# Graph network kernel on one Trainium2 core: message sums into two column halves of TensorE, a 128-partition accumulator, and a merged, pipelined node update

## What is computed

```
layer 0:  g = (h @ W) * dis ;  agg = segment_sum(g[src], dst) ;  x += h + gelu(dis * (agg + g) + b)
layer 1:  msg = relu([h[src], h[dst], edge] @ W1 + b1) @ W2 + b2
          agg = segment_sum(msg, dst)
          x  += relu([agg, h] @ U1 + c1) @ U2 + c2
```

## Time and profile before

| | us |
|---|---|
| median of 3 runs | 2646.51 |
| the three runs | 2646.51, 2634.43, 2647.69 |
| the profiled execution, its own time | 2642.74 |
| its span, first to last instruction | 2641.0 |
| busy: PE, PE weight loads, DVE, POOL, ACT | 2303.5, 1988.5, 1827.3, 1829.3, 1130.6 |

### The profile page before, as it was taken

The page is one execution under the profiler, slowest core; times in us unless marked ns, Lnnn a source line. Parts: engine busy times, 40 slices in busy tenths (PEclk is TensorE's granted clock), DMA queues, the critical chain, the costliest instruction groups (busy, mean ns, idle before and its releaser), DMA issues.

```text
span 2641.0 us, 71244 instructions
## 1 busy us (share of the span) xinstructions
PE 2303.5 (87%) x22534; PEld 1988.5 (75%) x22535; DVE 1827.3 (69%) x5068; ACT 1130.6 (43%) x2326; POOL 1829.3 (69%) x1684
## 2 busy tenths in 40 slices
PE   2357999999994499999999999999999999999988
PEld 1246778777873378888888888888888888888874
DVE  8876777777786676666666666666666666666642
ACT  0016778878883133333333333333333333333321
POOL 2647777777770067777777777777777777777770
PEclk7569999999997699999999999999999999999986
DMA  2011111111120323333233333233223333332331
GB/s 65 1 27 27 27 28 27 28 28 28 28 28 2 71 50 64 66 65 65 63 64 65 66 65 65 65 65 65 64 63 65 66 66 66 66 65 65 64 49 24
DMA packets 349624, 134.26 MB, mean 51 GB/s; under 512 B 306107, under 2 KB 323361, under 8 KB 349473
## 3 DMA queue, kind: packets, MB, share of 16 engines
q1 hardware_dynamic: 297506, 79.11, 13.3%
q0 software_dynamic: 51968, 53.32, 10.8%
HBM read 124.78 MB, written 7.49 MB: 50 GB/s over the span
## 4 chain that ended last, share of the span: by engine, by line
PE 34%; POOL 32%; issue 13%; DVE 10%; DMA 6%; SPq 3%; ACT 1%; DVEq 1%; POOLq 0%; PEldq 0%; ACTq 0%
POOL rows L573 32%; PE psum L1306 8%; PE psum L1337 6%; PE psum L1458 4%; PE psum L1423 3%; DMA rows<-a_rows,idx 3%; PE psum L1432 2%; DMA idx<-src_by_tile 2%; PE psum L1470 2%; PE psum L1443 2%; PE psum L1327 2%; DVE H L949 1%; SPq L445 1%; PE psum L1414 1%; PE psum L1515 1%
## 5 line engine op out<-in xcount | busy, mean ns | idle before, releaser
L573 POOL DMA_INDIRECT rows<-a_rows,idx x1176 | 1284.1, 1092 | 496.0 <-issue 337.7
L573 POOL DMA_INDIRECT rows<-g_rows,idx x448 | 463.1, 1034 | 169.4 <-issue 135.0
L1115 ACT ACTIVATE hT<-psum 128x392 bf16<-128x392 f32 x1120 | 496.7, 502 | 139.2 <-PE psum L1337 131.8
L949 DVE TENSOR_SCALAR H<-Y,node_cmp 128x512 bf16<-128x512 f16 (+1 forms) x1372 | 383.0, 353 | 192.8 <-ACT Y L1150 192.8
L1458 PE MATMUL psum<-edge_index,H 128*128 128x192 bf16 x4802 | 430.3, 247 | 32.0 <-DVE H L949 32.0
L1306 PE MATMUL psum<-work,hT 128*128 128x192 bf16 x3430 | 447.1, 248 | 0.3 <-ACT hT L1115 0.3
L1458 PEld LDWEIGHTS psum<-edge_index,H 128*128 128x128 bf16 x4802 | 397.1, 99 | 54.9 <-issue 52.2
L1337 PE MATMUL psum<-Z,one_lo 128*128 128x392 f16 x1120 | 359.3, 342 | 28.8 <-DVE Z L827 28.6
L1423 PE MATMUL psum<-wb,eoT 128*128 128x64 f32 x3136 | 380.3, 275 | 0.0
L1306 PEld LDWEIGHTS psum<-work,hT 128*128 128x128 bf16 x3430 | 317.7, 99 | 70.6 <-issue 3.5
L1423 PEld LDWEIGHTS psum<-wb,eoT 128*128 128x128 f32 x3136 | 368.9, 193 | 0.1
(11 more groups left out here) (237 smaller groups left out, 2140.3 us busy)
## 6 DMA issues: line engine op xcount, KB each, us to landing
work<-in_edge_attr_dram SPq DMA_DIRECT2D x390, 128.0 KB
rows<-a_rows,idx POOLq DMA_INDIRECT x1176
Z<-slot_code SPq DMA_DIRECT2D x98, 128.0 KB, 3.0
rows<-g_rows,idx POOLq DMA_INDIRECT x448
idx<-src_by_tile SPq DMA_DIRECT2D x203, 4.0 KB, 1.8
wb<-b_rows SPq DMA_DIRECT2D x196, 16.0 KB, 1.9
g_rows<-Y SPq DMA_DIRECT2D x1, 1600.0 KB, 7.1
a_rows<-Y SPq DMA_DIRECT2D x1, 1600.0 KB, 7.2
```

The costliest lines, as they stand in the source:

```text
L573: pool.indirect_dma_start(out=rows[:, k, t, :], out_offset=None, in_=table, in_offset=bass.IndirectOffsetOnAxis(ap=idx[:, k, t:t + 1], axis=0)
L949: ins = V.tensor_scalar(pick[:, b, cols], slot_src[:, cols], node_cmp[:, b:b + 1], None, ALU.is_equal)
L1115: nc.scalar.activation(counts[:, j % 2, :, t * SLOTS:(t + 1) * SLOTS], psum[:, t % 4, 0:KEYS].rearrange("p (h m) -> p h m", m=SLOTS), ACT.Copy
```

## The change

1. `sum_messages` sums the even tiles into partitions 0 to 63 of the PSUM bank and the odd ones into 64 to 127, in the same sixteen weight loads and matmuls. `acc` has 128 partitions, and DVE's addition takes all of them.
2. The node update has two stages. `w_agg` is `w_msg2 @ w_upd1[0:64]`, stacked twice (so that it also adds the two halves) and repeated in both column halves; `w_node` holds `w_upd1[64:128]` for `h`, and in row 0 `b_msg2 @ w_upd1[0:64]` for the count of edges, which is now row 0 of `hT`. The hidden layer comes out twice, on 128 partitions, and `w_out` is half of `w_upd2`, stacked twice. Hidden and output products follow each other in one loop, two chunks apart, and SP stores each eight blocks as they are ready.
3. The merged weights are made in the preparation, behind layer 0's table: a transpose and two products on PE, seven small copies on ACT. SP's list of weights grows from 11 to 15 DMAs.
4. The output bias is added to `X` by DVE between the layers, in the place where DVE cleared `acc`. POOL clears the upper part of `hT` and the 128 partitions of `acc` there, while the layer's first steps run, and SP reads the counts back there instead of in the preparation.

```diff
-        w_msg2 = sb("w_msg2", [D + 1, D])
-        w_upd1 = sb("w_upd1", [P, D])
-        b_upd1 = sb("b_upd1", [D, 1])
-        w_upd2 = sb("w_upd2", [D + 1, D])
+        w_msg2 = sb("w_msg2", [D, D])
...
+        w_node = sb("w_node", [P, P])
+        w_agg = sb("w_agg", [P, P])
...
-        acc = sb("acc", [D + 1, NP])
+        acc = sb("acc", [P, NP])
@@ SyncE
-            sp.wait_ge(s_acc0, 1)
-            sp.dma_start(acc[D:D + 1, :], cnt_dram.rearrange("(a b) p -> a (b p)", a=1)).then_inc(s_cntr, 16)
...
+            sp.wait_ge(s_hrow, 1)
+            sp.dma_start(hT[0:1, :], cnt_dram.rearrange("(a b) p -> a (b p)", a=1)).then_inc(s_cntr, 16)
             sp.wait_ge(s_codec, 1)
...
-            sp.wait_ge(s_u3c, NB // T + 1)
-            sp.dma_start(out[0:NFULL * P, :].rearrange("(b p) d -> p b d", p=P), Y[:, 0:NFULL, :]).then_inc(s_out, 16)
+            for c in range(0, NB, T):
+                sp.wait_ge(s_u3c, c // T + 1)
+                full = min(T, NFULL - c)
+                if full > 0:
+                    sp.dma_start(out[c * P:(c + full) * P, :].rearrange("(b p) d -> p b d", p=P), Y[:, c:c + full, :]).then_inc(s_out, 16)
@@ GpSimd
             nc.gpsimd.memset(acc[:, :], 0.0).then_inc(s_acc0, 1)
+            nc.gpsimd.memset(w_node[0:D, :], 0.0).then_inc(s_acc0, 1)
...
+            pool.wait_ge(s_stT, 1)
+            nc.gpsimd.memset(hT[0:D, :], 0.0).then_inc(s_hrow, 1)
+            pool.wait_ge(s_stT, NB // T + 1)
+            nc.gpsimd.memset(acc[:, :], 0.0).then_inc(s_acc1, 1)
             pool.wait_ge(s_mode1, 1)
@@ VectorE
-                        V.tensor_tensor(acc[0:D, bass.ds(b0, W)], acc[0:D, bass.ds(b0, W)], psum[0:D, 4, 0:W],
+                        V.tensor_tensor(acc[:, bass.ds(b0, W)], acc[:, bass.ds(b0, W)], psum[:, 4, 0:W],
...
-            link(V.memset(acc[0:D, :], 0.0))
+            bu3 = wide(b_upd2[:, :].rearrange("p (b d) -> p b d", b=1), 1, NB)
+            link(V.tensor_tensor(X[:, :, :], X[:, :, :], bu3, ALU.add))
+            dve.wait_ge(s_acc1, 1)
             dve.wait_ge(s_split_a, 2)
...
-            for c in range(0, NP, 512):
-                m = min(512, NP - c)
-                q = c // 512
-                dve.wait_ge(s_u1, q + 1)
-                V.tensor_copy(hT[0:D, c:c + m], psum[0:D, q % 2, 0:m]).then_inc(s_u1c, 1)
-
-            dve.wait_ge(s_u1, NP // 512 + 1)
-            V.memset(acc[D:D + 1, :], 1.0).then_inc(s_one_row, 1)
@@ ScalarE
             sqrt_var(0)
+            act.wait_ge(s_wT, 1)
+            for half in (slice(0, D), slice(D, 2 * D)):
+                nc.scalar.activation(w_msg2T[:, half], psum[0:D, 7, 0:D], ACT.Copy).then_inc(s_wTc, 1)
+            act.wait_ge(s_wagg, 1)
+            for half in (slice(0, D), slice(D, 2 * D)):
+                nc.scalar.activation(w_agg[:, half], psum[:, 7, 128:128 + D], ACT.Copy).then_inc(s_wready, 1)
+                nc.scalar.activation(w_node[0:1, half], psum[0:1, 7, 256:256 + D], ACT.Copy).then_inc(s_wready, 1)
+            nc.scalar.activation(w_out[:, :], w_upd2[:, :], ACT.Copy, scale=0.5).then_inc(s_wready, 1)
...
-                nc.scalar.activation(acc[0:D, c:c + m], psum[0:D, 2 + q % 2, 0:m], ACT.Relu, bias=b_upd1[:, :]).then_inc(s_u2c, 1)
+                nc.scalar.activation(acc[:, c:c + m], psum[:, q % 4, 0:m], ACT.Relu, bias=b_upd1[:, :]).then_inc(s_u2c, 1)
@@ TensorE
+            TT.transpose(psum[0:D, 7, 0:D], w_msg2[:, :], ident[0:D, 0:D]).then_inc(s_wT, 1)
+            pe.wait_ge(s_wTc, 2)
+            TT.matmul(psum[:, 7, 128:128 + D], w_msg2T[:, :], w_upd1[:, :], start=True, stop=True)
+            TT.matmul(psum[0:1, 7, 256:256 + D], b_msg2[:, :], w_upd1[:, :], start=True, stop=True).then_inc(s_wagg, 1)
+            pe.wait_ge(s_wready, 5)
...
-                        ins = TT.matmul(psum[0:D, 4, 0:W], msg[:, k % 2, t, :], eo[:, k, t, D:2 * D],
-                                        start=(t == 0), stop=(t == T - 1))
+                        half = (t % 2) * D
+                        ins = TT.matmul(psum[half:half + D, 4, 0:W], msg[:, k % 2, t, :], eo[:, k, t, D:2 * D],
+                                        start=(t < 2), stop=(t >= T - 2))
...
+            def hidden(c):
...
+                TT.matmul(psum[:, q % 4, 0:m], w_node[:, :], hT[:, c:c + m], start=True, stop=False)
+                TT.matmul(psum[:, q % 4, 0:m], w_agg[:, :], acc[:, c:c + m], start=False, stop=True).then_inc(s_u2, 1)
+
+            def output(b):
...
+                ins = TT.matmul(psum[:, 4 + c % 2, (b % T) * D:(b % T + 1) * D], acc[:, b * P:(b + 1) * P], w_out[:, :],
                                 start=True, stop=True)
...
+            hidden(0)
+            hidden(512)
+            for c in range(0, NP, 512):
+                if c + 1024 < NP:
+                    hidden(c + 1024)
+                for b in range(c // P, min(NB, (c + 512) // P)):
+                    output(b)
```

More of the change, by code:

```diff
@@ L57, in gnn_two_layers @@
     ADDS = MB + MS
+    NWT = 15
     KPE = 2
@@ L107, in gnn_two_layers @@
         b_msg1 = sb("b_msg1", [P, D])
-        w_msg2 = sb("w_msg2", [D + 1, D])
-        w_upd1 = sb("w_upd1", [P, D])
-        b_upd1 = sb("b_upd1", [D, 1])
-        w_upd2 = sb("w_upd2", [D + 1, D])
+        w_msg2 = sb("w_msg2", [D, D])
+        b_msg2 = sb("b_msg2", [D, 1])
+        w_msg2T = sb("w_msg2T", [D, P])
+        w_upd1 = sb("w_upd1", [D, D])
+        w_node = sb("w_node", [P, P])
+        w_agg = sb("w_agg", [P, P])
+        b_upd1 = sb("b_upd1", [P, 1])
+        w_upd2 = sb("w_upd2", [P, D])
+        w_out = sb("w_out", [P, D])
+        b_upd2 = sb("b_upd2", [P, D])
         edge_index = sb("edge_index", [P, 3, COLS])
@@ L277, in gnn_two_layers @@
         s_aclr = sem("s_aclr")
-        s_one_row = sem("s_one_row")
+        s_wT = sem("s_wT")
+        s_wTc = sem("s_wTc")
+        s_wagg = sem("s_wagg")
+        s_wready = sem("s_wready")
+        s_acc1 = sem("s_acc1")
+        s_hrow = sem("s_hrow")
         s_turn = [sem("s_turn_pool"), sem("s_turn_sp"), sem("s_turn_dve"), sem("s_turn_pe")]
@@ L386, in _ @@
                     for w_to, w_from in (
[L387 to L389 removed]
+                            (w_l0[:, :], l0_w), (w_msg2[:, :], msg_w2), (b_msg2[:, :], msg_b2.rearrange("(d a) -> d a", a=1)),
+                            (w_upd1[:, :], upd_w1[0:D, :]), (w_node[D:2 * D, 0:D], upd_w1[D:2 * D, :]),
+                            (w_node[D:2 * D, D:2 * D], upd_w1[D:2 * D, :]),
+                            (w_upd2[0:D, :], upd_w2), (w_upd2[D:2 * D, :], upd_w2),
+                            (b_upd2[:, :], wide(upd_b2.rearrange("(a d) -> a d", a=1), 0, P)),
+                            (b_upd1[0:D, :], upd_b1.rearrange("(d a) -> d a", a=1)),
+                            (b_upd1[D:2 * D, :], upd_b1.rearrange("(d a) -> d a", a=1)),
                             (w_ab[D:2 * D, 0:D], msg_w1[0:D, :]), (w_ab[D:2 * D, D:2 * D], msg_w1[D:2 * D, :]),
@@ L1509, in _ @@
             pe.wait_ge(s_cntr, 16)
-            for c in range(0, NP, 512):
+            HB = 512 // P
+            def hidden(c):
                 m = min(512, NP - c)
                 q = c // 512
-                if q >= 2:
-                    pe.wait_ge(s_u1c, q - 1)
-                TT.matmul(psum[0:D, q % 2, 0:m], w_msg2[:, :], acc[:, c:c + m], start=True, stop=True).then_inc(s_u1, 1)
-            for c in range(0, NP, 512):
-                m = min(512, NP - c)
-                q = c // 512
-                pe.wait_ge(s_u1c, q + 1)
-                if q >= 2:
-                    pe.wait_ge(s_u2c, q - 1)
-                TT.matmul(psum[0:D, 2 + q % 2, 0:m], w_upd1[:, :], hT[:, c:c + m], start=True, stop=True).then_inc(s_u2, 1)
-            pe.wait_ge(s_u2c, NP // 512 + 1)
-            pe.wait_ge(s_one_row, 1)
-            for b in range(NB):
+                if q >= 4:
+                    pe.wait_ge(s_u2c, q - 3)
+                TT.matmul(psum[:, q % 4, 0:m], w_node[:, :], hT[:, c:c + m], start=True, stop=False)
+                TT.matmul(psum[:, q % 4, 0:m], w_agg[:, :], acc[:, c:c + m], start=False, stop=True).then_inc(s_u2, 1)
+            def output(b):
                 c = b // T
@@ L1528, in _ @@
                     pe.wait_ge(s_u3c, c - 1)
-                ins = TT.matmul(psum[:, 4 + c % 2, (b % T) * D:(b % T + 1) * D], acc[:, b * P:(b + 1) * P], w_upd2[:, :],
+                if b % HB == 0:
+                    pe.wait_ge(s_u2c, b // HB + 1)
+                ins = TT.matmul(psum[:, 4 + c % 2, (b % T) * D:(b % T + 1) * D], acc[:, b * P:(b + 1) * P], w_out[:, :],
                                 start=True, stop=True)
```

12 lines of the change are left out of this document (6 added, 6 removed).

## The result

The changed kernel takes 2509.86 us (median of four runs, 2508.87 to 2512.91) against 2644.01 for the kernel before: a ratio of 0.9502, 95% interval 0.9484 to 0.952. The profiled execution took 2512.91 us with a span of 2511.1. I had said 2598, and 2575 to 2628. The kernel is faster, and by nearly three times what I forecast.

A forecast was written before the change was run, and what follows sets the result against it. The prediction took POOL's gathers to bound the message loop, by 1.5 us a turn over PE. Its terms, 2642.74 - 21 - 21.3 - 3.1, gave 2597.3, stated as 2598 us, range 2575 to 2628.

The forecast's parts named there:

- DVE's addition runs on 128 partitions instead of 64, with the same 64 columns, and is costed at nothing: Message loop: widening DVE's accumulator addition adds no time; if longer, DVE's 2.68 us wait at k = 1 would mostly cover it.
- whatever it gets shorter, POOL is released earlier, once a turn: Message loop: only the k = 1 sum lies on the path; 0.45 us saved in 47 turns gives 21 us.
- rival B: Message loop: the long gather vanishes because DVE's run shifts in phase; turn 30.2 to 30.4 us, total 2472; chance 0.07.
- The sum in two halves: PE's message sum: loads and products of the two halves overlap, so sixteen matmuls take 0.69 us instead of 1.15.
- A: Message sum: the halves do not overlap, or POOL hides what they save; 2618 us; chance 0.36.
- D: Message sum: each change of half drains PE, making the kernel slower, up to 3035 us; chance 0.05.
- The node update: Kernel's end: two-stage products at mostly the higher clock take 37.4 us, then 4.0 us to finish; 21.3 us saved.
- C: Kernel's end: stays at 1.2 GHz, +4 us instead of -21.3; 2623 us with the sum's gain, 2644 without; chance 0.05.
- Between the layers: Between the layers: an addition to X replaces DVE's clearing of acc, starting the next subtraction earlier; 3.1 us saved.

The follow-up runs named there:

- e14: Kernel before, with only DVE's accumulator addition widened to 128 partitions (upper PSUM half cleared to zeros), sum still in one half; 2567.7 us, ratio 0.9721.
- e7: Changed kernel with all tiles summed into one half and the addition on 64 partitions; 2623.5 us, ratio 0.9921.
- e9: Changed kernel with the addition on 64 partitions, halves still alternating, odd tiles' messages left out; 2525.2 us, ratio 0.9571.
- e8: Changed kernel with a step's first four tiles summed in the lower half, last four in the upper, addition on 128 partitions; 2523.7 us, ratio 0.9544.
- e5: Changed kernel plus a one-element VectorE write on partitions 0 to 63 behind each accumulator addition; 2501.1 us, ratio 0.9449.
- e15: Changed kernel with the end's output products contracting 64 rows in place of 128; 2512.1 us, ratio 0.9498.
- e17: e8 with the addition on 96 partitions in every step; 2581.7 us, ratio 0.9784.
- e16: e8 with the addition on 64 partitions in steps k = 2 and on 128 in the others; 2563.2 us, ratio 0.9701.
- e1: Same edit as e7 on a slow chip: changed kernel, sum in one half, addition on 64 partitions; 3933.8 us beside 3954.1 for the kernel before.
- e3: Same edit as e9 on a slow chip: changed kernel, halves alternating, addition on 64 partitions; 3943.0 us beside 3954.1 for the kernel before.
- e4: Kernel before with 2052 unused bytes per partition ahead of the edge index, shifting later buffers; slow chip, 3967.1 us beside 3954.1 for the kernel before.
- e11: e8 with the addition on 128 partitions in steps k = 2 alone and on 64 in the others; slow chip, no time given.
- e13: e7 plus a one-element VectorE write on all 128 partitions behind each accumulator addition; slow chip, no time given.
- e18: The changed kernel itself, unedited, run on a slow chip; 4021.9 us, ratio 0.9979 against the kernel before.

## Why the prediction was wrong, step by step

**The step that failed** is "DVE's addition runs on 128 partitions instead of 64, with the same 64 columns, and is costed at nothing". The instruction itself does cost nothing (0.21 us as before), but with it goes the long gather, POOL's hold over the loop. That is worth 76 us (49 x (33.49 - 31.94)) by e14, and nothing in the sum stood for it. I had asked only how long it takes, not what it does to the engine beside it. The Trainium skill's "SBUF — State Buffer", section Who interferes with whom, has the frame: VectorE and GpSimd share a port pair as an exclusive lock. By that page the lock is held for one instruction, and it has no rule in which the number of partitions counts. The trace does not agree: here a gather was held over eleven instructions, and the partitions of an earlier one decided.

**The second failed step** is "whatever it gets shorter, POOL is released earlier, once a turn", 21 us. With the addition still on 64 partitions (e7 to e9) the faster sum gave 98 us: in most turns the run moved from 0.1 to 0.6 us behind a gather's start to 1.0 to 1.3, where the gather took 1.3 to 1.6 us and not 4, and the long gathers fell from 48 to 5. That is my rival B, by its own reason. I gave it 0.07 because line 949's run never held a gather, and because the run at k = 1 starts after a wait. Both observations were right, and the conclusion was not: a wait does keep the gather short (13 meetings of 13 in the kernel before), and so does the phase (46 of e9's 51 chains without a wait), and it was the phase that the faster sum could change. B's 2472 us were too low: I let the turn fall to 30.3, and at 31.2 PE and its wait for DVE take over. In the changed kernel, as it is, the width alone keeps the gathers short (51 of 51 met), and the halves give the other 36 us (49 x 0.74), since PE had become the bound.

**The sum in two halves** was right as one sum's length: 0.69 us said, 0.69 found, so loads and products of two column halves overlap though both have the same rows. Even two groups of four in turn (e8) took 0.97. The Trainium skill's "TensorE: Matmul & The Clock Gate", Part 3, says that a weight load overlaps running matmuls only where the row group differs; this trace does not agree. It does agree with the independent tiles of the Trainium skill's "TensorEngine Tiling (Array Packing)", section Key Properties. A and D fell with it.

**The node update** was right in mechanism: -21.3 said, -23.2 measured. A chunk's four products take 1.77 us (2485.36 to 2487.13) where I had 4 x 0.48 = 1.92, near the bound of 0.43 that I named; eight outputs 0.84 for 8 x 0.11. From the loop's last addition to the start of DVE's last ones it is 35.4 us where I had 37.4 to PE's last product, and what comes after is 4.6 for my 4.0. C fell: no stretch at 1.2 GHz later on.

**Between the layers** was right and looked like nothing. From DVE's addition to `X` that opens the stage (line 1038, now 1060)

```profile
829.81 3.48 DVE L1060 TENSOR_TENSOR X<-X,H 128x3200 f32<-128x3200 f32 x1
```

to the first gather it is 917.54 - 829.81 = 87.7 us; before it started at 826.72, 90.8 us. That is the 3.1. But layer 0 ended 3.1 us later. e14, the same code as before up to there, starts it at 823.57, and e5, e7 to e9 and e15 to e17, the same as the changed kernel, between 826.3 and 831.5. So layer 0's end moves by some microseconds without a cause in the code, and it stays open how much of the 3.1 is the longer preparation (SP's issues take 4.2 us more; PE's line 1369, before 1337, starts 0.6 us later).

**The sum of the terms**: said 21 + 21.3 + 3.1 = 45; found 76 (not in it) + 36 + 23 + 3, less 3 of layer 0 and some 5 in the loop's first and last turns. The range had no room for B, and its chance should have been far more: I had seen two meetings of run and gather, one held and one not, which differed in the wait and in the distance, and had settled on the wait.

## What to carry to other kernels

When a GpSimd gather takes four times its usual length, put its start beside VectorE's instructions for many turns and ask both what the distance is and what VectorE did just before. Here a VectorE instruction on part of the partitions, ahead of a chain without a pause, cost 78 us of 2645, and filling it up to 128 partitions with zeros was the whole cure. And when one engine's stall goes, read the next bound's need from the profile before multiplying a saving by its count.

## What the hardware showed

- Width and the held gather: with the addition on 64 or 96 partitions and no pause behind it, a gather begun 0.1 to 0.6 us before the run is long in 160 of 165 meetings on the first chip (before, e7, e9, e16, e17), until the eleven instructions are through. On the slow chips it is 185 of 198 (e1, e3, e4, e11, e13). These are all the long gathers that the traces have. With a pause of any length between addition and run it is none of 91. With the addition on 128 partitions it is none of 283 on the first chip (changed, e5, e8, e14, e15, e16) and none of 212 on the slow ones; in 12 of these 495, all at a distance of 0.12 to 0.13 us, the gather took 2.17 us, until the seven were through, and never longer. Two full-width instructions stand between the addition and the run. What inside the engines keeps this, no record shows: it is shown which instruction decides, not why.
- When such a gather is not held, the run of seven pays instead: 2.16 to 2.30 us on the first chip in place of 1.91.
- Two chips run every version at 1.5 times the time. On the slower of them the change gives nothing: the changed kernel 4021.9 us, ratio 0.9979 (0.9951 to 1.0007). PE there in e18:

```profile
2416.66 0.24 PE L1491 MATMUL psum<-edge_index,H 128*128 128x192 bf16 x1 [1.17 <-issue]
2417.39 0.24 PE L1491 MATMUL psum<-edge_index,H 128*128 128x192 bf16 x1 [0.48 <-issue]
2418.82 0.32 PE L1491 MATMUL psum<-edge_index,H 128*128 128x192 bf16 x1 [1.18 <-issue]
```

Matmuls that follow each other at once on the first chip have 0.5 to 1.2 us of idle time between them, with nothing recorded that they wait for; "issue" has 20% of the chain that ended last against 8% on the first chip. VectorE's, ScalarE's and GpSimd's instructions last as long as there. PE's do so only in part: its granted clock over the loop is 0.78 against 1.00, and a matmul of line 1455 takes 366 ns in the mean against 275. What slows the issue is open, and so is how much the lower clock adds; a gain that comes from one engine's stall is hidden under it.
